# One semaphore set for the halves and one for the tags of each expert tile, the tags loaded one tile later

## The reference, cut

```
h = h + attn(_layernorm(h))
t = _layernorm(h).reshape(-1, 128)
hs = gelu(einsum('td,nfd->ntf', t, sw1) + sb1);  shared = einsum('ntf,ndf->td', hs, sw2) + sb2.sum(0)
probs = softmax(t @ gate_w.T + gate_b);          top_v, top_i = top_k(probs, 2)
cw = zeros_like(probs).at[arange(T)[:, None], top_i].add(top_v)
hr = gelu(einsum('td,efd->etf', t, rw1) + rb1);  oe = einsum('etf,edf->etd', hr, rw2) + rb2
h = h + shared + einsum('etd,te->td', oe, cw)
```

## Time and profile before

| | us |
|---|---|
| median of 3 runs | 1250.35 |
| the 3 runs | 1245.68, 1250.35, 1252.90 |
| profiled execution, its own time | 1243.88 |
| span of the profiled execution | 1242.2 |
| PE busy in the span | 1169.7 (94%) |
| DVE busy | 970.1 (78%) |
| POOL busy | 840.9 (68%) |
| ACT busy | 807.6 (65%) |
| first tile's load issued by SP | 744.40 |
| last tile's first product on PE | 1091.60 |

### The profile page before, as it was taken

One profiled execution on the slowest core, in us unless ns is written; L12 is line 12 of the kernel. 1 busy time (PEld: TensorE's weight loads), 2 busy tenths in 40 slices (PEclk: granted clock), 3 DMA queues, 4 the chain that ended last, 5 costly groups with the idle time before them and its releaser, 6 DMA issues.

```text
span 1242.2 us, 32105 instructions
## 1 busy us (share of the span) xinstructions
PE 1169.7 (94%) x9514; PEld 886.8 (71%) x9514; DVE 970.1 (78%) x2516; ACT 807.6 (65%) x1867; POOL 840.9 (68%) x808
## 2 busy tenths in 40 slices
PE   4999999999999999868999988999999999999998
PEld 2777777777777777644555447999999889964555
DVE  5688898888888888757987765777777767778997
ACT  2566666666665566535555545777777777768877
POOL 4435776666677776546887784777777777776564
PEclk8999999999999999979999998999999999999999
DMA  6233444444444442223444424544555444439998
GB/s 179 81 113 115 129 132 132 131 132 126 119 134 128 131 121 74 67 73 101 112 114 128 111 62 88 98 97 99 93 95 92 92 97 96 90 81 189 204 201 165
DMA packets 208056, 143.53 MB, mean 116 GB/s; under 512 B 119036, under 2 KB 186745, under 8 KB 207892
## 3 DMA queue, kind: packets, MB, share of 16 engines
q1 hardware_dynamic: 166868, 93.93, 30.1%
q0 software_dynamic: 36992, 40.97, 15.4%
q10 hardware_dynamic: 4032, 6.57, 2.1%
HBM read 70.38 MB, written 55.96 MB: 102 GB/s over the span
## 4 chain that ended last, share of the span: by engine, by line
PE 33%; POOL 32%; issue 24%; SPq 4%; DMA 3%; ACT 3%; DVE 1%; POOLq 0%; ACTq 0%; DVEq 0%
POOL slots_dram L483 9%; POOL slots_dram L1544 4%; POOL y_dram L1555 4%; POOL rstd L524 3%; PE bank L1832 3%; PE bank L1856 3%; PE bank L1857 3%; PE bank L1855 3%; PE bank L1834 3%; PE bank L1833 3%; PE bank L1263 2%; POOL rstd L530 2%; PE bank L1264 2%; PE bank L1265 2%; PE bank L1304 2%
## 5 line engine op out<-in xcount | busy, mean ns | idle before, releaser
L1555 POOL DMA_INDIRECT y_dram<-y_sb,y_row x244 | 268.3, 1100 | 92.7 <-issue 74.1
L1640 ACT ACTIVATE gel_all<-bank,b 128x256 f32<-128x256 f32 x488 | 191.8, 475 | 49.7 <-PE bank L1834 47.7
L1271 ACT ACTIVATE gel_all<-bank,b 128x458 f32<-128x458 f32 x256 | 154.8, 640 | 83.5 <-PE bank L1265 56.2
L1855 PE MATMUL bank<-w_part_hi,hid_all 128*128 x976 | 170.5, 219 | 0.0
L1857 PE MATMUL bank<-w_part_hi,hid_all 128*128 x976 | 169.9, 219 | 0.0
L1856 PE MATMUL bank<-w_part_lo,hid_all 128*128 x976 | 169.9, 219 | 0.0
L1762 DVE CAST hid_all<-gel_all 128x1024 f16<-128x1024 f32 x122 | 85.6, 702 | 107.0 <-ACT gel_all L1640 107.0
L483 POOL DMA_INDIRECT slots_dram<-row_bufs,slot_1st x128 | 129.9, 1015 | 39.2 <-issue 39.2
L1764 DVE TENSOR_TENSOR hid_all<-gel_all,hid_all 128x1024 f16<-128x1024 f32 x122 | 149.5, 1225 | 4.2
L1544 POOL DMA_INDIRECT slots_dram<-row_bufs,slot_2nd x104 | 125.6, 1208 | 31.6 <-issue 31.0
L1282 DVE TENSOR_TENSOR hid_all<-gel_all,hid_all 128x916 f16<-128x916 f32 x128 | 142.4, 1113 | 4.4
(11 more groups left out here) (190 smaller groups left out, 3001.8 us busy)
## 6 DMA issues: line engine op xcount, KB each, us to landing
xin<-in_xmain SPq DMA_DIRECT2D x32, 771.8 KB
x2r_dram<-row_bufs SPq DMA_DIRECT2D x32, 260.0 KB, 2.1
x2t_dram<-x2T SPq DMA_DIRECT2D x32, 229.0 KB, 2.9
row_bufs<-x2r_dram SPq DMA_DIRECT2D x26, 260.0 KB, 2.9
x_cols<-x2t_dram ACTq DMA_DIRECT2D x28, 229.0 KB, 2.8
stage<-in_ffn_w SPq DMA_DIRECT2D x20, 256.0 KB
xin<-in_xrest SPq DMA_DIRECT2D x32, 128.6 KB
y_dram<-y_sb,y_row POOLq DMA_INDIRECT x244
```

The costliest lines, as they stand in the source:

```text
L1271: act.activation(self.gel[:, f // 2 % 2, f % 2, :], self.up_dst(k, f), ACT.Gelu, bias=self.b1[:, f:f + 1]).then_inc(self.gel_ready, 1)
L1555: pool.indirect_dma_start(out=y_dram, in_=y_sb[:, s, c, :], in_offset=None, out_offset=bass.IndirectOffsetOnAxis(ap=y_row[:, s, c:c + 1], ...
L1640: act.activation(gel[:, s8 % 2, f, :], up_bank[s8 % 2][half][:, (f % 2) * TILE:(f % 2 + 1) * TILE], ACT.Gelu, bias=of_expert(b1, SHARED * ...
L1855: pe.matmul(part, h_hi, w2_hi, start=False, stop=False)
```

## The change

The two loads of a tile get semaphores of their own, four of each kind: `tile_in[t % 4]` for the halves and `tags_in[t % 4]` for the tags. `load_tile` issues the halves alone and waits for `up_done` of tile t - 4; a new `load_tags` reads the tile's first row a second time, waits for `row_set` of tile t - 4 and `y_ready` of tile t - 8, and issues the tags. In SP's loop the tags of tile t - 1 come behind the halves of tile t. PE's `up` waits for the halves, DVE's `y_rows` for the tags, and ACT's `out_y` has one more wait, on `row_set`.

```
+    IN_SEMS = 4
...
-        tile_in = [sem(f"tile_in{n}") for n in range(TILE_BUFS)]
+        tile_in = [sem(f"tile_in{n}") for n in range(IN_SEMS)]
+        tags_in = [sem(f"tags_in{n}") for n in range(IN_SEMS)]
...
             def load_tile(t):
                 b = t % TILE_BUFS
                 at = sp.value_load(tile_base[0:1, t:t + 1], min_val=0, max_val=SPARE)
+                if t >= IN_SEMS:
+                    sp.wait_ge(up_done, 2 * (t - IN_SEMS + 1))
+                sp.dma_start(xT[:, b], slots_16[bass.ds(at, TILE), 0:2 * HID], transpose=True).then_inc(tile_in[t % IN_SEMS], 16)
+
+            def load_tags(t):
+                b = t % TILE_BUFS
+                at = sp.value_load(tile_base[0:1, t:t + 1], min_val=0, max_val=SPARE)
+                if t >= IN_SEMS:
+                    sp.wait_ge(row_set, t - IN_SEMS + 1)
                 if t >= TILE_BUFS:
-                    sp.wait_ge(up_done, 2 * (t - TILE_BUFS + 1))
-                    sp.wait_ge(row_set, t - TILE_BUFS + 1)
                     sp.wait_ge(y_ready, t - TILE_BUFS + 1)
-                sp.dma_start(xT[:, b], slots_16[bass.ds(at, TILE), 0:2 * HID], transpose=True).then_inc(tile_in[b], 16)
                 sp.dma_start(tags[:, b], slots_dram[bass.ds(at, TILE), HID:].rearrange("(c p) w -> p c w", p=P)
-                             ).then_inc(tile_in[b], 16)
+                             ).then_inc(tags_in[t % IN_SEMS], 16)
...
             for t in range(TILES):
                 load_tile(t)
+                if t > 0:
+                    load_tags(t - 1)
                 if t == TILE_BUFS - 1:
...
+            load_tags(TILES - 1)
...
             def out_y(t, s8):
                 act.wait_ge(down_done, t + 1)
+                act.wait_ge(row_set, t + 1)
...
             def y_rows(t, s8):
-                dve.wait_ge(tile_in[s8], 4 * (t - s8) + 32)
+                dve.wait_ge(tags_in[s8 % IN_SEMS], 16 * ((t - s8 % IN_SEMS) // IN_SEMS) + 16)
...
             def up(t, s8, e, f):
                 if f == 0:
-                    pe.wait_ge(tile_in[s8], 4 * (t - s8) + 32)
+                    pe.wait_ge(tile_in[s8 % IN_SEMS], 16 * ((t - s8 % IN_SEMS) // IN_SEMS) + 16)
```

## The result

The changed kernel took 1301.80 us in the median of 4 runs (1297.00 to 1303.37), the one before 1251.62 (1245.68 to 1255.05): 4.1% slower, ratio 1.0405 with a 95% interval of 1.038 to 1.0429. The profiled execution took 1303.37 us with a span of 1301.6, against 1243.88 and 1242.2 before, 59.5 us more.

What follows compares the result with a forecast made beforehand. SP's DMA-issuing queue was taken to set the tile stage's pace after the change: 72.0 - 0.6 - 2.9 = +68.5 us on 1243.88 gives 1312.4, plus 2 makes 1314 us. Its own range was 1304 to 1326, with rival 1 1296 to 1326.

Steps and rivals of the forecast that it cites:

- The bound and the mechanism: Tile stage: SP's queue has no pause, the second table read adds to it, PE waits at every tile; 66%.
- Rival 2: Tile stage: SP isn't the bound, its issuing steps are covered by transfers and the extra read costs nothing; 1240.4 us, 5%.
- The term of the reads: SP's queue: 120 added table reads of 0.60 us before the last halves, +72.0 us, and one tags load fewer, -0.6 us.
- The lead: Last tile: SP's lead over PE shrinks from 5.87 us to a halves' landing of 3.0 us, -2.9 us.
- The rest of the program: After the last tile's first product: same work, 150.6 us; POOL's slack might bring 1 or 2 us, left at zero.
- The base: Whole program: the sum starts from the profiled 1243.88 us; 2 us added because the earlier runs' median was 1250.35.
- Rival 1: SP's tile stage: its 20.6 us of long issues shrink; 1292 us if all vanish, 1302 if half do; 25%.
- Rival 3: PE in the tile stage: idling brings the half clock for a fifth of the stage, +50 us, 1362 us; 4%.
- The removed wait: PE's first product waiting for halves alone: worth at most 9.5 us in the stage, some 0.6 at tile 0; none counted.

## Why the prediction was right, and where it was off

**The bound and the mechanism held.** SP's queue had no pause before, the second table read goes on top of it, PE waits for halves (the view has such a wait at 50 tiles, where the forecast had one at every tile; PE was busy for 87% of the stage, 295.5 of 340 us, and not for 80%), and the slowdown is there with the read alone (1306.5 us) and gone without it (1243.9). The chain of work now runs over SP. Rival 2, that SP's issuing steps don't count, is refuted by the run with three reads and by the one with a read in one tile of four. The point, 1314 us, was 12 us too high; the range held.

**The term of the reads was too large.** It had 0.60 us a tile, +72.0 and -0.6. SP's stage grew by 60.0 us, 0.496 a tile, so that this term was 11 us too high. The rows tell which step: in the gap between the two issues, 1147.03 - (1144.99 + 1.22) = 0.82 us against 0.20 before, the read and the semaphore step that moved there take 0.62; behind the tags' issue, 1148.13 - (1147.03 + 0.39) = 0.71 us against 0.80; and the tags' issue itself has 0.39 against 0.42. That is 0.62 - 0.09 - 0.03 = 0.50. With the semaphore step of 0.05 taken off, the read was 0.57 us, the lower bound that I had given, and the semaphore step was only moved. The two kernels with nothing but a second read agree: 0.77 - 0.20 = 0.57 us between the issues, 1.33 - 0.80 = 0.53 in front of the halves.

The other 0.06 to 0.07 us, 8 us in the stage, are the part that was priced wrong: I took all other instructions of SP at their old price. Over the whole stage the tags' issue fell from 0.475 to 0.410 us in the mean, half of it because its ordinary time fell from 0.42 to 0.39 and half because long ones became rarer, and the rest came off the gap behind it. It isn't the distance from the transposing issue that makes an ordinary tags' issue cheaper: it takes 0.39 us too in the kernel with one read, where only 0.26 us lie between the two. What does is open.

**The lead.** I expected PE 3.0 us behind SP at the last tile, -2.9 us; it was 4.44, -1.4. At tile 0 it was 750.06 - 746.85 = 3.21, so that the landing of the halves was sized well, but a late one at the end cost a microsecond and a half. **The rest of the program** gave 1.6 us, of the 1 to 2 that I had named and left at zero; POOL's slack is there, 83.3 us of waits for ACT.

**The base.** The sum was made on a profiled execution of 1243.88 us, which the later runs show to be near the fast end of the kernel before (1242.4 to 1255.5), while the profiled execution after, 1303.37, was the slowest of its four. Between the two profiles lie 59.5 us, between the medians 50.2. I added 2 us because the median of before lay above its profile. The runs of the changed kernel lie at or below theirs: 1297.0 to 1303.4.

**Rival 1**, long issues that shrink with a longer stage, came about in a small part. What the stage takes beyond its undisturbed tiles stayed: 401.3 - 121 x 3.14 = 21 us after, 20.6 before, and 463.0 - 121 x 3.68 = 18 us with three reads. But this remainder also holds the slow ones among the table reads, of which there are now more. The two issues of a tile by themselves took 1.78 us in the mean before and 1.72 after, some 6 us less over the stage; 1.66 to 1.71 in the three other kernels with two or three reads in every tile; and 1.74 to 1.85 in the others with one. That is part of the 12 us by which the point was too high. These are single traces, and those with one read differ by as much among themselves. Taking the scatter away didn't remove the long issues. What makes an issue of 1.22 us take 2 is open.

**Rival 3**, the clock, came about in a small way and cost nothing. Apart from its first tiles, which ran at half clock as in the kernel before, the changed kernel had the granted clock at half for one short stretch of the stage, after PE had been busy for 2.12 of 4.00 us:

```profile
1096.00:1100.00 4.00, 2.12 (x30) 1.70 (x28) 2.73 (x4) 2.23 (x6) 3.06 (x4) 1.00 0.64 87
1100.00:1103.40 3.40, 3.23 (x18) 2.44 (x19) 0.45 (x1) 1.19 (x3) 1.58 (x2) 0.50 0.40 90
1103.40:1110.00 6.60, 6.60 (x96) 6.31 (x93) 4.06 (x7) 4.88 (x14) 3.22 (x3) 1.00 0.34 69
```

PE fell further behind SP there and caught up again, since it has 3.14 - 2.76 = 0.4 us a tile to spare. From 756 to 1096 us, with PE busy for 295.5 of 340 us, the clock stayed full.

**The removed wait** had been put at 9.5 us at most and at nothing in the sum. The nothing holds. The 9.5 was misread: it took the 2.76 us between two first products for PE's pace over the whole stage, whereas PE that never waits for a load in the stage takes 339.1 us and not 334.0, so that the stage before (343.5) had lost 4.4. The rows had it: of the 10.2 us of waits for tags, 6.7 stand before tile 0, which leaves 3.5 in the stage. With the second read gone the gain is 0.3 to 0.4%, 4 to 6 us, and the profiled execution has nothing left to gain from SP.

## What to carry to other kernels

A queue that only issues DMAs has no busy time in a profile; compare the distance of its issues in the timeline with the pace of the engine that it feeds, and look whether it ever waits. If it never does, each of its register steps costs its full time, and a table read is one of the dear ones. When one load is split into two, keep the address in a register for the second; and count what is added to the busy queue: the version with the split and a single read gained 4 to 6 us here, and one read too many in each of 122 tiles cost ten times that.

## What the runs showed of the hardware

- Reading a word from on-chip memory into a register on SP, with its range arithmetic, takes 0.53 to 0.57 us a time in undisturbed tiles: TENSOR_LOAD 274 ns, FUSED_REGOPS 157, SEQ_ASSERT 18 and three gaps. In none of the places where it was put (between the two issues, in front of the halves, twice in a row) was it hidden behind the DMA issued before it.
- The issue of a transposing DMA holds SP for 1.22 us and that of a small plain one for 0.39 to 0.42. At tile 0 PE started 3.21 us after the start of the first (changed kernel) and 748.07 - 745.93 = 2.14 us after the start of the second (kernel before). Both have long issues, up to 2.3 and 1.6 us in the kernel before, together some 16 us over its 122 tiles; when SP isn't ahead of the engine that it feeds, they are the likely source of most of the run-to-run spread of 13 us.
- Half clock in single stretches of 3.4 us cost nothing here, where another engine set the pace: the stage of the kernel with three reads has eight of them behind its first tiles, and in it SP waits for PE once, for 0.3 us.
